# One more semaphore wait ahead of the first exponential of every key tile

## The reference

```
q = (hidden_states @ Wq.T + bq).reshape(b, s, HEADS, HEAD_DIM)     # 16 heads of 16
k, v = ...                                                         # the same with Wk, Wv
scores = jnp.einsum('bqhd,bkhd->bhqk', q * SCALE, k)
probs = jax.nn.softmax(scores.astype(jnp.float32), axis=-1)
out = jnp.einsum('bhqk,bkhd->bqhd', probs, v).reshape(b, s, d)
return out @ Wo.T + bo
```

## Time and profile before

| | |
|---|---|
| median of three runs | 3143.73 us |
| the profiled execution | 3143.73 us |
| its span, first to last instruction | 3142.0 us |
| PE busy | 3092.5 us, 98% |
| DVE busy | 2868.2 us, 91% |
| ACT busy | 2450.2 us, 78% |
| granted TensorE clock, mean | 0.995 |

### The profile page before, as it was taken

How to read it: one execution, slowest core, us unless ns; L and a number is a source line. 1 busy time by engine, 2 the same in 40 slices (tenths; PEclk the granted TensorE clock), 3 DMA queues, 4 the chain that set the end, 5 groups by cost and what they waited for, 6 DMA issues and landing times.

```text
span 3142.0 us, 73284 instructions
## 1 busy us (share of the span) xinstructions
PE 3092.5 (98%) x23912; PEld 1570.4 (50%) x23912; DVE 2868.2 (91%) x4046; ACT 2450.2 (78%) x4631; POOL 947.8 (30%) x1403
## 2 busy tenths in 40 slices
PE   7999999999999999999999999999999999999998
PEld 6544444444444444444444444444444444688887
DVE  7758999999999999999999999999999999466666
ACT  3557888888888888888888888888888888544443
POOL 2551222222222222222222222222222232344444
PEclk9999999999999999999999999999999999999999
DMA  5685333333333333333333333333333331455554
GB/s 198 197 236 101 59 59 59 59 59 59 65 63 62 64 63 63 61 59 59 59 59 59 59 59 59 64 63 65 63 64 60 59 75 39 140 160 164 164 161 127
DMA packets 139857, 271.93 MB, mean 87 GB/s; under 512 B 30144, under 2 KB 75264, under 8 KB 127296
## 3 DMA queue, kind: packets, MB, share of 16 engines
q1 hardware_dynamic: 137472, 266.71, 40.3%
q10 hardware_dynamic: 2112, 1.35, 0.2%
HBM read 173.59 MB, written 84.93 MB: 82 GB/s over the span
## 4 chain that ended last, share of the span: by engine, by line
PE 91%; DMA 0%; DVE 0%; issue 0%; SPq 0%; ACT 0%; POOL 0%; POOLq 0%; DVEq 0%; ACTq 0%
PE a_ps L917 35%; PE s_ps L907 34%; PE m_ps L899 8%; PE o_ps L1186 6%; PE h_ps L1176 5%; PE inv_ps L1209 1%; DMA mask_bc<-mask_b 0%; PE inv_ps L1196 0%; PE o_ps L1217 0%; DMA att_dram<-att 0%; SPq L1093 0%; DVE base L1326 0%; SPq L1100 0%; POOL g_lo L1410 0%; DVE z L1299 0%
## 5 line engine op out<-in xcount | busy, mean ns | idle before, releaser
L983 DVE TENSOR_REDUCE half_max<-m_ps 128x1 f32<-128x1024 f32 x3009 | 2369.5, 860 | 10.0 <-PE m_ps L899 9.8
L867 ACT ACTIVATE prob<-s_ps 128x512 f32<-128x512 f32 x4096 | 2128.3, 602 | 290.7 <-PE s_ps L907 290.6
L907 PE MATMUL s_ps<-q_feat,k_feat 50*128 50x512 f32 x4096 | 1444.1, 450 | 2.4 <-ACTq L859 2.4
L899 PE MATMUL m_ps<-k_feat,q_feat 48*128 48x512 f32 x4012 | 1341.2, 434 | 0.3 <-DVE half_max L983 0.3
L917 PE MATMUL a_ps<-prob,v_head 128*32 128x512 f32 x12280 | 1202.3, 463 | 3.9 <-issue 3.9
L907 PEld LDWEIGHTS s_ps<-q_feat,k_feat 50*128 50x128 f32 x4096 | 681.9, 184 | 896.3 <-ACT prob L867 834.5
L899 PEld LDWEIGHTS m_ps<-k_feat,q_feat 48*128 48x128 f32 x4012 | 648.5, 185 | 14.4 <-DVE half_max L983 1.1
L917 PEld LDWEIGHTS a_ps<-prob,v_head 128*32 128x32 f32 x12280 | 243.1, 108 | 472.3 <-issue 453.4
L704 POOL COPY v_head<-v_all 128x256 f32 (+1 forms) x64 | 25.3, 397 | 826.9 <-PE a_ps L917 826.8
L1257 ACT ACTIVATE g_hi<-g 128x512 fp32r<-128x512 f32 x128 | 81.0, 633 | 213.5 <-DVE g L1290 173.0
L711 POOL CAST shift<-row_max 128x16 fp32r<-128x16 f32 x63 | 12.3, 195 | 759.2 <-DVE row_max L985 759.2
(11 more groups left out here) (145 smaller groups left out, 2010.5 us busy)
## 6 DMA issues: line engine op xcount, KB each, us to landing
q_feat<-q_parts SPq DMA_DIRECT2D x384, 128.0 KB, 4.3
k_feat<-k_parts SPq DMA_DIRECT2D x384, 128.0 KB, 5.7
q_parts<-parts SPq DMA_DIRECT2D x32, 512.0 KB, 4.3
k_parts<-parts SPq DMA_DIRECT2D x32, 512.0 KB, 4.3
att_dram<-att SPq DMA_DIRECT2D x64, 256.0 KB, 6.3
mask_bc<-mask_b SPq DMA_DIRECT2D x128, 128.0 KB, 4.4
x_in<-in_x SPq DMA_DIRECT2D x16, 512.0 KB, 4.4
xn_dram<-xn SPq DMA_DIRECT2D x16, 512.0 KB, 5.0
```

The lines of the kernel that those rows point to most:

```text
L867: act.activation(prob[tile(r, kt) % R][:, cols(j)], s_ps[slot(r, kt, j) % R][:, :], ACT.Exp).then_inc(exped, 1)
L899: pe.matmul(m_ps[j // 2][:, (j % 2) * BLK:(j % 2 + 1) * BLK], q_feat[r % 2][LOW, qt * P:(qt + 1) * P], k_feat[r % 2][LOW, j * BLK:(j + 1) ...
L907: pe.matmul(s_ps[slot(r, kt, j) % R][:, :], k_feat[r % 2][UP, kt * P:(kt + 1) * P], q_feat[r % 2][UP, cols(j)], start=True, stop=True).the ...
L983: dve.tensor_reduce(half_max[r][:, qt, o:o + 1], max_source(m_ps, o), AX.X, ALU.max).then_inc(maxed, 1)
```

## The change

Ahead of the first exponential of each key tile (`j == 0`) ACT now also waits for `weighed >= tile(g, kt) + 1`, that is, until the weigh of tile T-3 is done. The waits for `parts_stored`, once in the program, move from slot (1,0) of the first head under the same condition and stand behind the new wait. No computation is added, removed or moved; there are 1024 new waits, one for each of 64 x 16 tiles.

```diff
             def exp(g, r, kt, j, first=False):
-                if first and (kt, j) == (1, 0):
-                    for done in parts_stored:
-                        act.wait_ge(done, 16 * NBLK + 16)
+                if j == 0:
+                    act.wait_ge(weighed, tile(g, kt) + 1)
+                    if first and kt == 1:
+                        for done in parts_stored:
+                            act.wait_ge(done, 16 * NBLK + 16)
                 act.wait_ge(scored, slot(g, kt, j) + 1)
                 act.activation(prob[tile(r, kt) % R][:, cols(j)], s_ps[slot(r, kt, j) % R][:, :],
                                ACT.Exp).then_inc(exped, 1)
```

## The result

The changed kernel takes 3170.67 us (median of 6 runs, 3168.56 to 3171.98) against 3143.6 us of the kernel before (6 runs, 3138.1 to 3146.31). The ratio is 1.0091, 95% interval 1.0081 to 1.0102: 27 us slower. The forecast was no change, 3144 us, with 3138 to 3156 as its range. It was wrong.

A forecast was written before the change was run, and what follows sets the result against it. The prediction took PE's order of work to set each pair of key tiles (4.73 us), with DVE following and ACT having room. All added costs were hidden and summed to 0 us: 3144 us, range 3138 to 3156.

The forecast's parts named there:

- The new condition is never the last to be met: At all 1024 places `weighed` comes ahead of `scored`, by 0.42 us (even tiles) or 0.71 us (odd); cost zero.
- The wait for `scored` moves off the ACTIVATE and costs a detour: At each tile's first exponential, a separate wait on ACT starts it 0.12 us after the score instead of 0.04: 0.08 us.
- The rival that the detour does not happen: A separate wait costs ACT nothing when its condition is met in time; exponential (6,0) unmoved, 3144 us; chance 0.10.
- Even tiles hide it: Exponentials (even,0) to (even,2) start 0.08 us later; tightest spare 0.12 us, at score (odd,1); cost 0.
- Odd tiles hide it, 0.27 us between, 0.15 spare: ACT is busy until 0.27 us after score (odd,0) ends; the separate wait needs 0.12; cost 0.
- Its first sign of being wrong: The pair grows, and the lag of exponential (odd,0) behind its score has reached what ACT's own pace allowed.
- Tile 2 hides it: Behind each head's copy to `att`, 0.14 us lie between score (2,0) and its exponential; 0.12 needed, 0.02 spare; cost 0.
- The sum: All costs together 0 us on a span of 3142.0 and a time of 3143.73; forecast 3144 us.
- The slower rival: At the even tile's first exponential, an extra beyond 0.12 us delays score (odd,1) and PE: some 13 us, 3157; chance 0.18.
- Its upper case: PE's slack is not there at all, so the full 0.08 x 512 = 41 us is paid: 3185 us.
- the faster rival: Later exponentials let PE's pieces fall closer together, up to 0.05 x 512 = 26 us: 3118 us; chance 0.08.

The follow-up runs named there:

- e3: Changed kernel with its two waits exchanged, so the ACTIVATE carries the score's wait and the 1024 waits for the weigh stand separate: 3143.50 us.
- e4: Kernel before with the added wait for the weigh at slot 1 of every tile instead of slot 0, the score's wait separate: 3145.39 us.
- e2: Kernel before with the added wait for the weigh at slot 0 of even tiles alone: 3142.30 us.
- e5: Kernel before with the added wait for the weigh at slot 3 of even tiles alone (512 places): 3162.03 us.

## Why the prediction was wrong, point by point

- *The new condition is never the last to be met.* Right. e3 holds the same condition at all 1024 places and takes as long as the kernel before. In the semaphore records `weighed` steps at 1487.063 for tile 7, 0.90 us ahead of `scored`, and in the changed kernel it is at least 0.39 us ahead at every tile from the fourth on.
- *The wait for `scored` moves off the ACTIVATE and costs a detour.* Right in kind; the size was 0.06 us, forecast 0.08. This was named as the whole effect of the change, and it is. The rival that the detour does not happen is refuted by the same rows; what it named as its ground, a condition met in time, is what makes e3 and e4 cost nothing.
- *Even tiles hide it.* Right (e2). Gaps of 0.33 and 0.25 us, forecast 0.35 and 0.24.
- *Odd tiles hide it, 0.27 us between, 0.15 spare.* **This step failed.** The spare time was zero. 0.27 us was measured from the modelled end of a matmul, which is not when PE signals it: the semaphore steps only behind the key products ahead of it in PE's order, 0.244 us later. The exponential stood 0.022 us behind it. The forecast had itself called this cover the one that matters most, and had seen that score (odd,3) follows without slack; with the right release time its own sum would have read 0.08 x 512 = 41 us, and with the measured size 0.06 x 512 = 31 us, where 27 were measured. Its first sign of being wrong, a pair that grows while (odd,0) has lost its room, named the right place.
- *Tile 2 hides it.* Right: the tile's own exponential (2,0) starts 0.137 us after its score's end as before. Its pair still grew, through tile 3.
- *The sum.* The starts of the scores (even,0), as means over heads 2 to 58, give the growth of the eight pairs of a head: 0.065, 0.065, 0.066, 0.068, 0.067, 0.064, 0.004 and 0.046 us, 0.445 together; times 63 it is 28 us. Six pairs pass on their 0.06, and the last two do not pay it in full. In the kernel before, score (odd,3) starts 0.053 us (median) behind the end of exponential (odd,0) in the first six pairs, but 0.093 and 0.090 in the seventh and eighth; in the changed kernel it is 0.053 in all eight. So in those two pairs something other than ACT held PE, and some 0.04 us of slack took up part of the detour. What held it is not shown.
- *The rivals.* The slower rival named the right cause, a detour that outgrows its cover, but put it at the even tile and beyond 0.12 us. Its upper case, no slack at all and 3185 us, is the nearest to what happened: the slack was missing at the odd tile, the detour was 0.06 instead of 0.08, and two pairs of eight paid less. The range stopped at 3156. Nothing of the faster rival showed in the changed kernel. A rule of the Trainium skill bore on just this and was not weighed: TensorE: Matmul & The Clock Gate ("Why this matters for your kernels") states in a table row on semaphore increments that concurrent matmuls complete in exact program order. The semaphores' steps agree: 0.244 us of lag with the key product ahead, 0.016 with it behind. The modelled ends of the rows do not keep that order: score (7,0) ends 0.20 us before the key product ahead of it.
- A sign stood in rows of the kernel before. ACT's own pace is 0.48 to 0.49 us ((6,0) starts at 1485.59 and (6,2) at 1486.56, so 0.97 for two), but exponential (7,0) came 0.51 us after (6,3), and 0.07 us after the last key product, whose row ends at 1487.29 + 0.63 = 1487.92:

```profile
1487.29 0.63 PE L899 MATMUL m_ps<-k_feat,q_feat 48*128 48x512 f32 x2
```

An exponential that starts later than ACT's pace allows may be waiting for something, however busy ACT looks; here it was.

## What to carry to other kernels

Of two waits ahead of one instruction, let the instruction carry the one that is met last. Here that is the one written first, and exchanging two lines was worth 27 us. Do not read the slack behind a matmul from the end of its row: where matmuls ran side by side here, each was signalled in the order of the program, so look for the last one ahead of it; and place the product that another engine waits for ahead of those that nobody waits for yet. In a loop where two engines hand over without slack, even 0.06 us is paid at nearly every turn.

## What the runs showed of the hardware

- A matmul's semaphore can step 0.244 us after the matmul's modelled end, because of products ahead of it in the order that use other rows of the array. With nothing ahead still running it was 0.014 to 0.016 us. Steps that were held back follow each other 0.034 us apart.
- A wait in an instruction of its own costs ACT 0.061 us between the semaphore's step and the start (0.083 against 0.022) at (odd,0); at (even,0) and, in e5, at (even,3) it is 0.06 as well. Where its condition is met before ACT is free, the same instruction cost nothing (e3, e4: 1024 of them). In the project stage the wait on a register instruction cost 0.08.
- The order of the kernel before was not at its best: 11 us, 0.31% (interval 0.19 to 0.43%), lay in one line's place.
